# Sparse attention stage of a hybrid model: gathered key rows are transposed before their rank rotation, and VectorE rotates them on the way out of PSUM

## What is computed

```python
c_kv = x @ W_dkv                                   # 32 latents a token
I = einsum('bths,h->bts', relu(q_i . k_i), idx_w)  # index scores, every pair of tokens
I = where(local, inf, I); I = where(future, -inf, I)
_, idx = top_k(I, 96)                              # 64 local tokens, then the 32 best others, in rank order
kr_sel = (x @ W_kr)[bi, idx]                       # 32 rotary features of each picked token
angles_k = arange(96)[:, None] * theta + delta     # the angle goes by the RANK, not by the token
key_r = _pope(kr_sel, angles_k)                    # mu1 cos - mu2 sin, mu1 sin + mu2 cos
scores = (q_c . k_c + q_r . key_r) * scale
out = softmax(scores) . v ;  out @ W_out
```

## Time and profile before

| what | us |
|---|---|
| median of 3 runs (1143.5 to 1151.66) | 1144.84 |
| the profiled execution | 1145.09 |
| its span, first to last instruction | 1143.1 |
| around the span | 2.0 |

### The profile page before, as it was taken

The page is one execution under the profiler, slowest core; times in us unless marked ns, Lnnn a source line. Parts: engine busy times, 40 slices in busy tenths (PEclk is TensorE's granted clock), DMA queues, the critical chain, the costliest instruction groups (busy, mean ns, idle before and its releaser), DMA issues. The chain is left out here.

```text
span 1143.1 us, 19761 instructions
## 1 busy us (share of the span) xinstructions
PE 982.3 (86%) x6714; PEld 723.2 (63%) x6714; DVE 816.7 (71%) x1752; ACT 684.6 (60%) x1761; POOL 588.5 (51%) x616
## 2 busy tenths in 40 slices
PE   6999999998989884897898878888989787879786
PEld 4888877665658433565665667666766676567443
DVE  3777874746464578979888889978798989633237
ACT  3666645645454653766667658865686676655345
POOL 2100023424243077767777777777777777775000
PEclk8999999998999865958688778988788988887689
DMA  7100001000000068233433243313322333231000
GB/s 235 41 1 1 1 1 42 1 1 1 0 1 1 1 157 198 51 76 84 115 70 70 63 105 69 68 40 69 69 64 47 70 70 71 64 81 34 0 1 37
DMA packets 58626, 62.07 MB, mean 54 GB/s; under 512 B 27872, under 2 KB 43168, under 8 KB 58016
## 3 DMA queue, kind: packets, MB, share of 16 engines
q1 hardware_dynamic: 42656, 36.41, 12.5%
q0 software_dynamic: 15872, 24.41, 10.2%
HBM read 52.65 MB, written 8.13 MB: 53 GB/s over the span
## 5 line engine op out<-in xcount | busy, mean ns | idle before, releaser
L758 POOL DMA_INDIRECT gathered_rows<-key_table,idx_T x496 | 492.1, 992 | 182.5 <-issue 149.1
L773 PE MATMUL bank<-index_k_hi,index_q 128*128 128x512 f32 (+5 forms) x160 | 81.4, 511 | 24.5 <-ACT index_relu L1704 15.0
L1192 PE MATMUL bank<-ident,rotated_rows 128*96 128x128 f32 x512 | 92.2, 311 | 4.6 <-DVE rotated_rows L2254 4.6
L1721 ACT ACTIVATE turned_rows<-bank 96x512 f32<-96x512 f32 x128 | 74.2, 580 | 35.2 <-PE bank L1192 35.0
L2222 DVE SCALAR_TENSOR_TENSOR index_sums<-index_relu,iw,index_sums 128x512 f32<-128x512 f32 (+5 forms) x120 | 77.6, 647 | 21.3 <-ACT index_relu L1704 16.8
L1732 ACT ACTIVATE probs<-probs,attn_columns 128x208 f32<-128x208 f32 x128 | 59.5, 465 | 55.6 <-DVE attn_columns L2272 54.7
L1704 ACT ACTIVATE index_relu<-bank 128x512 f32<-128x512 f32 (+5 forms) x160 | 76.9, 496 | 23.8 <-PE bank L773 21.8
L2254 DVE TENSOR_TENSOR rotated_rows<-gathered_rows,rank_rope 128x384 f32<-128x384 f32 x128 | 71.0, 555 | 26.1 <-DMA gathered_rows<-key_table,idx_T 25.6
L1727 ACT ACTIVATE probs<-masked_scores,attn_columns 128x208 f32<-128x208 f32 x128 | 59.5, 465 | 34.8 <-DVE attn_columns L2267 27.8
L1216 PE MATMUL bank<-ident,probs 128*128 128x128 f32 x128 | 42.5, 332 | 43.9 <-ACT probs L1732 43.5
L2231 DVE MAX8 top<-index_sums 128x8 f32<-128x96 f32 (+15 forms) x64 | 78.2, 1222 | 1.2
(11 more groups left out here) (279 smaller groups left out, 2538.5 us busy)
## 6 DMA issues: line engine op xcount, KB each, us to landing
queries_in<-q_rot SPq DMA_DIRECT2D x32, 256.0 KB, 4.2
gathered_rows<-key_table,idx_T POOLq DMA_INDIRECT x496, 2.5
q_rot<-rotated SPq DMA_DIRECT2D x16, 256.0 KB
queries_in<-q_lat SPq DMA_DIRECT2D x16, 256.0 KB, 5.3
h<-in_h SPq DMA_DIRECT2D x2, 1024.0 KB, 7.6
q_lat<-q_latent_sb SPq DMA_DIRECT2D x8, 256.0 KB, 3.3
local_values<-key_table SPq DMA_DIRECT2D x15, 80.0 KB
x<-in_xT SPq DMA_DIRECT2D x1, 1024.0 KB, 5.2
```

The lines of the kernel that those rows point to most:

```text
L758: pool.indirect_dma_start(out=G[b][:, q, :], out_offset=None, in_=key_table[0:index_width(i), :], in_offset=bass.IndirectOffsetOnAxis(ap=i ...
L773: return pe.matmul(out_, lhsT, rhs, start=start, stop=stop, **kw)
L1192: last = pe.transpose(bank[2][0:ROW, j * P:(j + 1) * P], GR[n % 2][:, j, :], ident[:])
L1721: fn(GT[n % 2], bank[2][0:ROW, :], ACT.Copy).then_inc(a_gts, 1)
```

## The change

The gathered rows are transposed as they come. `rank_rope` is stored transposed (96 partitions x 128), and VectorE multiplies by it while it takes the transposed rows out of PSUM bank 2 into `turned_rows` (96x512). ScalarE's `rows_copy` and the two buffers `rotated_rows` are gone. TensorE's `rows_turn(n+1)` now waits for the gather itself; VectorE's `rows_rotate` is for group n+1 instead of n+2, waits for TensorE's transposes of the same slot, and stands behind `sum_invert(n-1)` instead of ahead of it.

```diff
-    t["rank_rope"] = np.tile(row, (P // JG, 1)).astype(f32)
+    t["rank_rope"] = np.ascontiguousarray(np.tile(row, (P // JG, 1)).T).astype(f32)
...
             def rows_turn(n):
-                pe.wait_ge(a_rot, n + 1)
+                i, g = n // NG, n % NG
+                if n < FIXED // GQ:
+                    pe.wait_ge(fixed_rows, 16 * QD)
+                else:
+                    gathers = i // 2 + (i % 2 == 1 or g >= FIXED // GQ)
+                    pe.wait_ge(gathered[i % 2][g], 16 * GQ // QD * gathers)
                 if n >= 1:
                     pe.wait_ge(a_gts, n)
                 for j in range(4):
-                    last = pe.transpose(bank[2][0:ROW, j * P:(j + 1) * P], GR[n % 2][:, j, :], ident[:])
+                    last = pe.transpose(bank[2][0:ROW, j * P:(j + 1) * P], G[i % 2][:, 4 * g + j, :], ident[:])
...
-            def rows_copy(n):
-                act.wait_ge(a_gt, n + 1)
-                if n >= 2:
-                    act.wait_ge(a_s, n - 1)
-                fn(GT[n % 2], bank[2][0:ROW, :], ACT.Copy).then_inc(a_gts, 1)
...
             def rows_rotate(n):
-                i, g = n // NG, n % NG
-                if n < FIXED // GQ:
-                    dve.wait_ge(fixed_rows, 16 * QD)
-                else:
-                    gathers = i // 2 + (i % 2 == 1 or g >= FIXED // GQ)
-                    dve.wait_ge(gathered[i % 2][g], 16 * GQ // QD * gathers)
+                dve.wait_ge(a_gt, n + 1)
                 if n >= 2:
-                    dve.wait_ge(a_gt, n - 1)
-                v.tensor_tensor(GR[n % 2], G[i % 2][:, 4 * g:4 * g + 4, :],
-                                rank_rope[:].unsqueeze(1).to_broadcast([P, 4, ROW]), ALU.mult).then_inc(a_rot, 1)
+                    dve.wait_ge(a_s, n - 1)
+                v.tensor_tensor(GT[n % 2].rearrange("r (j p) -> r j p", j=4), bank[2][0:ROW, :].rearrange("r (j p) -> r j p", j=4),
+                                rank_rope[:].unsqueeze(1).to_broadcast([ROW, 4, P]), ALU.mult).then_inc(a_gts, 1)
...
                 for s in range(SLOTS):
                     n = s - ATTN_LAG
-                    if 0 <= n + 2 < GROUPS:
-                        rows_rotate(n + 2)
                     if 0 <= n - 1 < GROUPS:
                         sum_invert(n - 1)
+                    if 0 <= n + 1 < GROUPS:
+                        rows_rotate(n + 1)
```

More of the change, by code:

```diff
@@ L283, in hybrid_kernel @@
         QG = over("q_picked", [NG, P], parts=ROW)
-        GR = [over(f"rotated_rows{b}", [4, ROW]) for b in range(2)]
         GT = [over(f"turned_rows{b}", [C], parts=ROW) for b in range(2)]
@@ L398, in hybrid_kernel @@
         v_loaded = [sem(f"local_values_loaded{b}") for b in range(2)]
-        (a_rot, a_gt, a_gts, a_s, a_max, a_exp_s, a_pt, a_pts, a_pv, a_rsum, a_pn, a_otc, a_y, a_x) = (
+        (a_gt, a_gts, a_s, a_max, a_exp_s, a_pt, a_pts, a_pv, a_rsum, a_pn, a_otc, a_y, a_x) = (
             sem("attn_" + n) for n in (
-                "rows_rotated", "rows_turned", "rows_turned_copied", "scores", "max", "probs", "probs_turned",
+                "rows_turned", "rows_rotated", "scores", "max", "probs", "probs_turned",
                 "probs_copied", "values", "sum_inverted", "probs_normed", "out_copied", "projected",
@@ L1752, in topk @@
                     n = s - ATTN_LAG
-                    if 0 <= n + 1 < GROUPS:
-                        rows_copy(n + 1)
                     if 0 <= n - 1 < GROUPS:
```

## The result

| | median us | runs | lowest to highest |
|---|---|---|---|
| before | 1144.92 | 4 | 1143.5 to 1151.66 |
| after | 1159.55 | 4 | 1157.74 to 1160.6 |

The ratio is 1.0114, with a 95% interval of 1.0072 to 1.0156: slower by 1%, where 1139 us was forecast. The profiled execution took 1159.0 us, with a span of 1156.9 against 1143.1. Executions that took over 1.5% longer than the fastest of their kernel count as slow and are left out of every median and ratio here.

What follows compares the result with a forecast made beforehand. It took the gather stream to bound the attention's end, with consumers catching up at 1005 us. Consumers gain 14 and lose 8 us (-6), the stream gains 16; the later consumers set the end: 1145.1 less 6 is 1139 us, range 1125 to 1158.

Steps and rivals of the forecast that it cites:

- The room: From 1005 us, consumers no longer held by gathers finish 14 us earlier: five light slots at 2.9 us.
- The stream: GpSimd's gathers: no longer stretched by the rotation, they end 14 us earlier, plus 2.4 us for one group ahead.
- The rotation itself: VectorE before 1005 us: each rotation takes 0.13 us more reading PSUM; 11 us taken, bounds 0 and 15.
- The rotation behind the reciprocal: VectorE before 1005 us: rotation behind waits for exp costs 13 us, an earlier exp returns 19; net -6.
- The index sums: VectorE before 1005 us: its 16.8 us of waits for index sums shrink, taken as -5 us.
- ScalarE's copies: 66.7 us busy on an engine with 32% idle time; removing them gives no more gain than counted.
- The new wait for the transposes: VectorE at tile ends: 1.6 us in ten slots, half absorbed later in the slot; +8 us, bounds 0 to 27.
- the three terms for waits: VectorE before 1005 us: rotation behind the reciprocal -6, index sums -5, wait for transposes +8 us.
- the 8 of the sum: Consumers before 1005 us: the change adds 8 us, from 11 - 6 - 5 + 8.
- rival 2: Slot head blocks VectorE: no waits shrink, transposes' lateness hits it whole; 28 us before 1005 us, 1159 us; chance 0.17.
- Behind the attention nothing changes: Last stages, some 80 us behind the attention's end: the change leaves them as they are.
- the ring: Experiments' theory, tile ends: out_project, transposes, rotation, add_tile, scores wait in turn, a large part of the lost time.

Runs made afterwards that it cites:

- e10: Kernel before with add_tile moved behind the search steps of its slot; 1144.23 us, ratio to before 1.0018.
- e2: Kernel before with two tiny VectorE instructions added behind each rotation, about 0.15 us a slot; 1145.55 us, ratio to before 0.9999.
- e5: Kernel after with add_tile moved ahead of the rotation in VectorE's slot; 1140.36 us, ratio to before 0.9958.
- e12: Kernel after with add_tile ahead of the rotation, the same kernel as e5 run again; 1141.43 us, ratio to before 0.9981.
- e7: Kernel after with only 256 of the 512 columns rotated and taken out of PSUM; 1139.44 us, ratio to before 0.9950.
- e3: Kernel before with sum_invert(n-1) moved ahead of rows_rotate(n+2); 1149.52 us, ratio to before 1.0045.
- e6: Kernel after with a 96x512 SBUF copy into a scratch tile added on ScalarE ahead of probs_norm; 1166.12 us, ratio to before 1.0177.
- e11: Kernel after with add_tile ahead of the rotation and out_project behind the transposes; 1141.77 us, ratio to before 0.9974.
- e9: Kernel after with TensorE's out_project moved behind rows_turn(n+1), ahead of scores(n); 1154.94 us, ratio to before 1.0113.
- e8: Kernel after with the rotation put ahead of sum_invert(n-1) again; 1159.64 us, ratio to before 1.0148.
- e1: Kernel after with VectorE's rotation moved behind row_max(n) in the same slot; 1154.65 us, ratio to before 1.0083.

## Why the prediction was wrong

**The room (14 us): right.** From group 111 to 127 after gives back 12.7 us; e10 hid 13 of 15.5 us of shift, and e2 all of its 7.

**The stream (16 us earlier): the mechanism right, the size not, and then not what it met.** In after the rotation stretches no gather: in the 679 to 1051 us stretch the mean fell by 24 ns, not 43. The 43 ns had been given to the rotation whole; about a third of the stretching was its own. I had left out the index sums, which multiply two SBUF inputs too, and the stretched gather of the earlier trace rows was theirs (the last section). And I treated the stream as independent of the consumers, though its indices come from the search on VectorE: at a shift of 26 us and more GpSimd waits 6.3 and 5.35 us for `idx_T`, and its waits at the starts of tiles 3, 4 and 7 add 8.4 us. The last gather came at 1060.5, not near 1036. It no longer set the end, though: VectorE never waited for it. With `add_tile` first it comes at 1043.1 in e5 and 1038.3 in e12, counted from the first gather of before.

**The rotation itself (+0.13 us, 11 us taken): a little small.** It takes 0.68 us as forecast, which is 14 us up to group 111; with smaller things VectorE's work grew by 19. I had counted three quarters of it, since VectorE waits in a quarter of the slots; e7 shows that it counts nearly in full. By the estimate from the Trainium skill, VectorE: DVE Perf Modes, TRN2 errata (198 ns more), the rotation would have taken 0.75 us; the rows have 0.68. The same section of the Trainium skill states (N + 151) cycles at 0.96 GHz for a float32 `tensor_tensor` add, an estimate of 0.69 us for N = 512, and the rows agree.

**The rotation behind the reciprocal (-6): no gain.** This is the first step that failed: e3 alone has a shift of +1.6 us and is 3.7 us slower. I had put the 44.1 us that ScalarE waits for the reciprocal, in the main, down to its place behind the rotation. ScalarE did get it earlier (27.8 us in e3), but exp waits for the scores and for `row_max`, so little came back. **The index sums (-5): about right** (18.3 us of waits for 22.2, up to group 111).

**ScalarE's copies ("no more gain than counted"): not settled.** e6's median is 6.6 us above after's, and its attention stage is no longer.

**The new wait for the transposes (+8, bounds 0 to 27): this is the step that decided.** I had the place and the lateness (1.6 us at ten tile ends), and VectorE's own part came as forecast (10 us net). I named `add_tile` as held, but had ScalarE and TensorE wait only for `row_max(n)` behind it. I did not ask who waits for `add_tile` itself: `scores(n)` on TensorE, for the release of its PSUM bank, and behind it `values`, the index scores, ScalarE's `attn_out`. "Half is absorbed by waits that come later in the same slot" did not hold: the three terms for waits sum to -3 us, and the waits of VectorE up to group 111 grew by 12. Exchanging two instructions (e5, e12) removes 15 to 19 us of time, as much as the whole loss, and 19 to 22 us of VectorE's waits. Together with the work (19 us where 11 was taken) that is the difference between 31 us and the 8 of the sum.

After and the kernels made from it that change the order at the tile end alone fall in the order of TensorE's wait for `add_tile`, though not in proportion to it: 4 us (e5, e12) 1140 to 1141, 9.5 us (e11) 1142, 12 us (e9) 1155, 16 us (after, e8) 1159.6. The kernel e1 is outside it: a wait of 4 us, and 1155, with TensorE held at the transposes instead.

So rival 2 was right in its price (1159; its 28 us came as 31), its place (the slot behind `out_project`) and its condition (it decides from 14 us on). Its sign came too, though barely: VectorE's waits for TensorE at the rotation sum to 21.3 us up to the end of the attention (18.2 and 3.1), and the wait for exp is nearly as long as before. Only half of its mechanism was right: it had VectorE blocked, and part of the cost lies in TensorE held by VectorE. That the sum came so close is in part luck, since it had 15 us of work and 13 of waits, and the runs have 19 and 12 with a cause that it did not name. What speaks against it in the prediction, that in other slots the transposes were done when ScalarE came, is true and beside the point, since an exchange that matters at the tile ends alone takes the loss back.

**Behind the attention nothing changes: not quite.** Of the 18.4 us, 4.6 were given back there, where TensorE's granted clock was higher (last section).

Left open: how the 12 us of more waiting up to group 111 divide between the ring and the order of reciprocal and rotation, since in one kernel they act on each other; what the removed copy is worth; and why e9's executions lie so far apart (1145.5 to 1158.9).

The version to keep is e5. Its first batch puts it 0.1 to 0.7% below before, its second holds 1. That is a gain that can hardly be measured: shorter waits and an earlier last gather pay for VectorE's added work, and little remains.

## What to carry to other kernels

When an instruction gets a new wait, write down what is queued behind it on its own engine, and for each of those who waits for its result or for the buffer that it releases, the once-a-tile instructions above all: here a 0.27 us add, once in eight slots, held three engines. Put short instructions that release something to another engine ahead of a long one that has to wait. And a delay that the kernel has room for shows in no time: e10 hid 13 us. So look at the shift of a marked instruction against before, not at the end alone, or the next change finds the room used up; and count it from a marker ahead of the change, since here up to 8.8 us of it had nothing to do with the change.

## What the hardware showed that was not expected

**What stretches a gather.** The stretched gather of the earlier trace rows was not held by the rotation at 871.12, as the prediction says. VectorE's timeline of before has, just ahead of it:

```profile
870.46 0.75 DVE L2222 SCALAR_TENSOR_TENSOR index_sums<-index_relu,iw,index_sums 128x512 f32<-128x512 f32 x1
```

Laying every gather of both traces against VectorE's instructions, one pattern fits: if a product with two SBUF inputs (index sums, rotations, query rotations) began 0.05 us or more ahead of the gather and is still active 0.15 us into it, the gather ends 0.82 us after that instruction does (here 871.21 + 0.82 = 872.03; it ended at 872.02). Of 166 such meetings in both traces 156 ended so; of 62 with a product that began later, in the first 0.12 us of the gather or just ahead of it, 2 did. Of the 159 gathers over 1.0 us in both traces, 155 end 0.82 us, give or take 0.02, behind an instruction of VectorE. It is a pattern read from times; no run was made to test it, and it is not the whole rule: the first of the index sums (`tensor_scalar`, L2219, one SBUF input and a column) stretched 1 us or so in all as well. One in after, GpSimd's timeline and VectorE's:

```profile
583.29 1.46 POOL L757 DMA_INDIRECT gathered_rows<-key_table,idx_T  x1 [0.30 <-issue]
```

```profile
583.18 0.75 DVE L2218 SCALAR_TENSOR_TENSOR index_sums<-index_relu,iw,index_sums 128x512 f32<-128x512 f32 x1
```

583.93 + 0.82 is 584.75, its end. In these two traces a product that begins well inside a gather does not touch it. In e1 it can. There the index sums often follow straight behind the rotation, and seven gathers that start within the rotation end 0.82 us behind index sums that began 0.20 to 0.39 us after the gather, as here (606.91 + 0.82 is 607.73, its end):

```profile
605.56 0.69 DVE L2245 TENSOR_TENSOR turned_rows<-bank,rank_rope 96x512 f32<-96x512 f32 x1
605.78 1.95 POOL L757 DMA_INDIRECT gathered_rows<-key_table,idx_T  x1 [0.30 <-issue]
606.17 0.74 DVE L2218 SCALAR_TENSOR_TENSOR index_sums<-index_relu,iw,index_sums 128x512 f32<-128x512 f32 x1
```

Other gathers of e1 in the same place stay at 0.94 us, so what decides is open. All in all e1's gathers are stretched more (mean 1006 ns over all 496) than those of before (992 ns) or after (975 ns), though its rotation reads PSUM too: where VectorE's instructions fall against the starts of the gathers counts as much as what the rotation reads.

Of some 24 us of stretching before, about 8 were the rotation's, about 10 those of the index sums, the rest of query rotations and smaller ones; after, it is 15, none of it from the rotation:

```profile
611.43 0.69 DVE L2245 TENSOR_TENSOR turned_rows<-bank,rank_rope 96x512 f32<-96x512 f32 x1
...
611.60 0.94 POOL L757 DMA_INDIRECT gathered_rows<-key_table,idx_T  x1 [0.30 <-issue]
```

Here the rotation is active when the gather starts and until 612.12. There are 56 gathers in after that start within a rotation, and all took 0.94 or 0.95 us. The Trainium skill, SBUF — State Buffer, "Who interferes with whom", infers that `tensor_tensor` leaves the making of descriptors alone; the traces contradict that for this gather where both inputs are in SBUF (1.46 us against 0.94). This gather reads its indices `idx_T` from SBUF besides, and no run tells which of the two the product holds up. With one input in PSUM after agrees with the section's rule that a single SBUF input does not contend (0.94 us above).

**The clock in the last stages.** Behind the last `attn_out` the work is the same in all kernels. The busy time of these stages in before, after and e5, with the granted clock (the third figure from the end):

```profile
1064.20:1143.10 78.90, 58.41 (x178) 34.82 (x178) 36.45 (x63) 37.16 (x68) 0.00 (x0) 0.81 0.04 14
```

```profile
1082.60:1156.90 74.30, 53.07 (x178) 31.96 (x178) 36.45 (x63) 36.94 (x68) 0.00 (x0) 0.89 0.04 14
```

```profile
1061.10:1142.10 81.00, 61.02 (x178) 37.12 (x178) 36.53 (x63) 37.21 (x68) 0.00 (x0) 0.77 0.04 13
```

TensorE's mean granted clock in the same 178 matmul records was 0.81, 0.89 and 0.77, and the stages took 78.9, 74.3 and 81.0 us. Over the 14 profiled executions they take 74 to 75 us at 0.88 to 0.89, 78 to 79 at 0.80 to 0.82, and 80 to 82 at 0.75 to 0.79. These 7 us are as large as half the effect studied, so a difference of a few us in the end of two profiled executions is no measure of a change in the attention.
